# Transformer layer: the last chunk's queries in two parts of 256, and a later place for the weights' rounding

## What is computed

```python
x = x + attention(layernorm(x))          # 16 heads of 16, rope on q and k, causal, q/k/v/o biases
x = x + fp4_mlp(layernorm(x))            # 704 wide, silu(gate) * up, then down
# fp4_linear(x, w): x and w are rounded to FP4 (E2M1) in blocks of 16 with one scale each,
# and then multiplied in float32; the hidden layer h is rounded the same way before "down"
att = where(causal, q @ k.T / sqrt(16), -inf); y = softmax(att) @ v; attention = y @ Wo.T + bo
```

## Time and profile before

| | us |
|---|---|
| median of 3 runs | 1295.78 (1288.91, 1295.78, 1295.86) |
| the profiled execution's own time | 1292.66 |
| its span in the profile | 1290.9 |
| TensorE busy | 1203.7 (93%) |
| VectorE busy | 1093.9 (85%) |
| ScalarE busy | 755.4 (59%) |
| GpSimd busy | 476.9 (37%) |

### The profile page before, as it was taken

How to read it: one execution, slowest core, us unless ns; L and a number is a source line. 1 busy time by engine, 2 the same in 40 slices (tenths; PEclk the granted TensorE clock), 3 DMA queues, 4 the chain that set the end, 5 groups by cost and what they waited for, 6 DMA issues and landing times.

```text
span 1290.9 us, 40076 instructions
## 1 busy us (share of the span) xinstructions
PE 1203.7 (93%) x16718; PEld 669.9 (52%) x16718; DVE 1093.9 (85%) x2932; ACT 755.4 (59%) x1630; POOL 476.9 (37%) x501
## 2 busy tenths in 40 slices
PE   8679999899999899999999899989999999999967
PEld 7345454454555445545565465545645554545545
DVE  6799998889997998999469799899899999885366
ACT  5246776466565476575655457456656566676621
POOL 3945655544213132122345663311122123014345
PEclk9779999899999999999999999989999999999989
DMA  4735323302101101101044222121111200000000
GB/s 108 183 96 163 103 77 88 99 26 68 43 28 51 51 3 51 35 27 45 10 109 128 81 77 77 51 61 35 38 34 44 59 11 3 19 2 18 5 22 16
DMA packets 79504, 72.40 MB, mean 56 GB/s; under 512 B 25934, under 2 KB 65744, under 8 KB 79312
## 3 DMA queue, kind: packets, MB, share of 16 engines
q1 hardware_dynamic: 76296, 68.76, 19.7%
q10 hardware_dynamic: 3028, 1.09, 0.3%
HBM read 45.07 MB, written 24.35 MB: 54 GB/s over the span
## 4 chain that ended last, share of the span: by engine, by line
PE 60%; DVE 24%; DMA 4%; ACT 4%; issue 3%; POOL 3%; SPq 1%; ACTq 0%; POOLq 0%; DVEq 0%
PE bank L992 13%; PE bank L968 11%; PE bank L1004 10%; PE bank L947 10%; DVE piece_max L1371 8%; DVE bank L1368 7%; PE bank L1123 5%; PE bank L1063 4%; ACT prob L1257 3%; PE bank L1097 2%; PE bank L1071 1%; PE bank L1114 1%; DVE piece_max L1368 1%; DMA q_mem<-max_rows 1%; DMA a_mem<-in_L_attn_x 1%
## 5 line engine op out<-in xcount | busy, mean ns | idle before, releaser
L1257 ACT ACTIVATE prob<-bank 128x512 f32<-128x512 f32 (+3 forms) x1280 | 594.2, 541 | 269.7 <-PE bank L968 152.6
L1371 DVE TENSOR_REDUCE piece_max<-bank 128x1 f32<-128x512 f32 x768 | 487.3, 676 | 9.4 <-PE bank L947 7.9
L968 PE MATMUL bank<-q_mem,k_mem 99*32 99x512 bf16 (+12 forms) x5120 | 388.0, 344 | 15.5 <-DMA q_mem<-max_rows 11.3
L947 PE MATMUL bank<-k_mem,q_mem 96*32 96x512 bf16 (+14 forms) x5120 | 379.5, 346 | 10.3 <-DVE piece_max L1368 5.9
L992 PE MATMUL bank<-prob,V 128*32 128x512 f32 (+3 forms) x2560 | 294.8, 533 | 13.5 <-ACT prob L1257 9.1
L968 PEld LDWEIGHTS bank<-q_mem,k_mem 99*32 99x32 bf16 x5120 | 144.5, 97 | 166.7 <-issue 70.3
L947 PEld LDWEIGHTS bank<-k_mem,q_mem 96*32 96x32 bf16 x5120 | 134.1, 97 | 186.2 <-issue 104.4
L1596 POOL TENSOR_TENSOR c_mem<-c_mem 128x256 f32<-128x256 f32 (+2 forms) x74 | 85.4, 1155 | 380.1 <-DVE c_mem L1470 380.1
L1368 DVE CUSTOM_DVE_ANT_0 bank<-bank,past_keys 128x32 f32<-128x32 f32 (+15 forms) x512 | 208.1, 468 | 3.3 <-PE bank L947 3.2
L992 PEld LDWEIGHTS bank<-prob,V 128*32 128x32 f32 x2560 | 70.4, 110 | 65.8 <-ACT prob L1257 30.5
L973 PE MATMUL bank<-mask_kq,ident_h 128*32 128x64 bf16 (+3 forms) x2048 | 101.6, 201 | 0.0
(11 more groups left out here) (177 smaller groups left out, 1337.9 us busy)
## 6 DMA issues: line engine op xcount, KB each, us to landing
output_dram<-attn SPq DMA_DIRECT2D x28, 256.0 KB, 3.0
parts_dram<-a_mem SPq DMA_DIRECT2D x13, 512.0 KB, 3.8
q_mem<-parts_dram SPq DMA_DIRECT2D x32, 192.0 KB, 3.1
k_mem<-parts_dram SPq DMA_DIRECT2D x32, 192.0 KB, 3.6
q_mem<-parts_dram SPq DMA_DIRECT2D x32, 128.0 KB, 3.1
k_mem<-parts_dram SPq DMA_DIRECT2D x32, 128.0 KB, 3.4
c_mem<-in_L_attn_x SPq DMA_DIRECT2D x30, 128.0 KB, 2.2
out<-c_mem SPq DMA_DIRECT2D x30, 128.0 KB, 1.7
```

The costliest lines, as they stand in the source:

```text
L947: m = pe.matmul(b[COLUMNS * h:COLUMNS * (h + 1), of], q_rows(u)[0:TERM_ROWS, h, block * COLUMNS:(block + 1) * COLUMNS], k_rows(k0 // CHUNK ...
L968: mm = pe.matmul(b[k0:k0 + COLUMNS, since:CHUNK], k_rows(j // TPC, g)[:, h, first:first + COLUMNS], q_rows(u)[:, h, since:CHUNK], start=Tr ...
L1257: act.activation(prob[:, n % NP, off:CHUNK], bank_of("st", n)[:, off:CHUNK], ACT.Exp, scale=SCALE).then_inc(drained("st", n)[0], 1)
L1371: r = dve.tensor_reduce(most, scores, AX.X, ALU.max)
```

## The change

- The last chunk has 8 units in place of 4: units 28 to 31 are its four groups for queries 0 to 255, units 32 to 35 the same groups for queries 256 to 511. The first part sees 14 steps of 128 keys a unit, the second 16, all up to 256 queries wide; before there were 16 steps up to 512 wide.
- Queries and keys are dealt to `q_mem` and `k_mem` only once for both parts (`dealt`, `deal_of`); the maxima are made and placed for each part.
- The pieces on the diagonal are packed anew: 3 banks in the first part and 8 in the second, in place of 9 a unit; the other 48 pieces of a group are split 24 and 24.
- A tile of the last chunk waits for the four units of its own part (`tile_normalised`), so tiles 28 and 29 can start after units 28 to 31.
- In the last 8 units the steps may hold 5 banks in place of 3.
- `w` of SOONER_NS goes from 0 to -20000.

```diff
-SOONER_NS = dict(a=0, w=0, xn=10000, ...
+SOONER_NS = dict(a=0, w=-20000, xn=10000, ...
...
-    units = [(k, g) for k in range(CHUNKS) for g in range(NGROUPS)]
+    PARTS = 2
+    units = [(k, g) for k in range(CHUNKS - 1) for g in range(NGROUPS)]
+    queries = [(0, CHUNK)] * len(units)
+    for part in range(PARTS):
+        units += [(CHUNKS - 1, g) for g in range(NGROUPS)]
+        queries += [(part * CHUNK // PARTS, (part + 1) * CHUNK // PARTS)] * NGROUPS
...
-        steps += [(u, j, max(0, j - c * TPC) * P) for j in range((c + 1) * TPC)]
+        low, high = queries[u]
+        steps += [(u, j, max(low, (j - c * TPC) * P)) for j in range(c * TPC + high // P)]
...
+        blocks = list(range(queries[u][0] // COLUMNS, queries[u][1] // COLUMNS))
+        pieces += [(u, [(0, n, j * BANK, BANK, j, False)]) for n in blocks for j in range(c)]
+        while blocks:
+            of = [blocks.pop(0)]
+            for n in reversed(blocks):
+                if n != BLOCKS - 1 and sum((n_ + 1) * COLUMNS for n_ in of + [n]) <= BANK:
+                    of.append(n)
+            blocks = [n for n in blocks if n not in of]
...
+    dealt = CHUNKS * NGROUPS
+    def deal_of(u):
+        return u if u < dealt else u - NGROUPS * ((u - dealt) // NGROUPS + 1)
...
     def rehearse_probabilities():
+            in_flight = 5 if u >= len(units) - 2 * NGROUPS else ST_IN_FLIGHT
...
+    def units_of(t):
+        k, i = tiles[t]
+        return [u for u in range(k * NGROUPS, len(units)) if units[u][0] == k and queries[u][0] <= i * P < queries[u][1]]
-    def chunk_normalised(k):
+    def tile_normalised(t):
+        k, _ = tiles[t]
         if by_transfers(k):
             return [("y", k * NGROUPS // 2 + p) for p in range(NGROUPS // 2)]
-        return [("drain", "oT", k * NGROUPS + g) for g in range(NGROUPS)]
+        return [("drain", "oT", u) for u in units_of(t)]
...
             def probabilities():      # TensorE
-                        masked = j >= c * TPC
+                        masked = j * P >= c * CHUNK + queries[u][0]
...
-                            mm = pe.matmul(b[k0:k0 + COLUMNS, since:CHUNK], ..., q_rows(u)[:, h, since:CHUNK], ...)
+                            mm = pe.matmul(b[k0:k0 + COLUMNS, since:end], ..., q_rows(u)[:, h, since:end], ...)
...
             def probabilities():      # ScalarE
-                        act.activation(prob[:, n % NP, off:CHUNK], bank_of("st", n)[:, off:CHUNK],
+                        act.activation(prob[:, n % NP, off:end], bank_of("st", n)[:, off:end],
...
             def outputs():
-                    act.activation(attn[:, :], bank[O_BANK][:, :], ACT.Copy).then_inc(o_copied, 1)
+                    of = slice(*queries[u])
+                    act.activation(attn[:, of], bank[O_BANK][:, of], ACT.Copy).then_inc(o_copied, 1)
...
             def turn_output(b, u):
-                for i in range(TPC):
+                for i in range(queries[u][0] // P, queries[u][1] // P):
```

More of the change, by code:

```diff
@@ L371, in rehearse_maxima @@
             keys, own = sum(part[3] for part in parts), parts[0][5]
-            yield from plan.wait([("deal q", u, len(RUNS) - 1)] + ([("deal k", u, len(RUNS) - 1)] if own else [])
+            yield from plan.wait([("deal q", deal_of(u), len(RUNS) - 1)] + ([("deal k", deal_of(u), len(RUNS) - 1)] if own else [])
                                  + ([("place", u - 2, 2)] if u >= 2 else [])
@@ L408, in rehearse_values @@
             of = k - k % NCHUNKS + j // TPC
-            yield from plan.step("pe", ("pv", m), 1.67 * (CHUNK - off) + 26,
+            yield from plan.step("pe", ("pv", m), 1.67 * (queries[u][1] - off) + 26,
                                  [("drain", "st", GROUP * m + 3), ("drain", "v", (of * TPC + j % TPC) // PAIR)]
@@ L413, in rehearse_values, with turned_before @@
                 old = [("o store" if by_transfers(units[u - 1][0]) else "oT", u - 1)] if u else []
-                yield from plan.step("act", ("o copy", u), 493, [("pv", m)] + old)
+                yield from plan.step("act", ("o copy", u), 80 + 0.807 * (queries[u][1] - queries[u][0]), [("pv", m)] + old)
                 plan.start(rehearse_normalising(u), SOONER_NS["norm"])
         plan.give(O_BANK, ("o copy", len(units) - 1))
+    def turned_before(u):
+        return u > 0 and not by_transfers(units[u - 1][0])
     def rehearse_normalising(u):
@@ L422, in rehearse_normalising @@
             yield from plan.wait(old)
-            yield from plan.through(("oT", u), 440, "dve", 335, [("o copy", u)], old,
-                                    ("dve", ("recip", u), 170) + ((("drain", "oT", u - 1),) if g else ()))
+            share = PARTS if k == CHUNKS - 1 else 1
+            yield from plan.through(("oT", u), 440 / share, "dve", 60 + 275 / share, [("o copy", u)], old,
+                                    ("dve", ("recip", u), 70 + 100 / share) + ((("drain", "oT", u - 1),) if turned_before(u) else ()))
             return
@@ L487, in rehearse_tiles @@
             yield from plan.wait(until=lambda: not tiles_c or all(
-                name in plan.end for name in chunk_normalised(tiles[tiles_c[0]][0])))
+                name in plan.end for name in tile_normalised(tiles_c[0])))
             if tiles_c:
@@ L915, in sync_engine @@
             in_time(constants(), *(project(z) for z in range(len(pairs))), *(store_parts(z) for z in range(len(pairs))), *(key_ones(c) for c in range(NCHUNKS)),
-                    weights(), *(deal(u) for u in range(len(units))),
+                    weights(), *(deal(u) for u in range(dealt)),
                     *(place_maxima(sp, at, u) for u in range(len(units)) if not placed_by_scalar(u)),
@@ L1082, in turn_y @@
                 k, i = tiles[t]
-                for g in range(NGROUPS):
-                    at.wait_ge(*drained("oT", k * NGROUPS + g))
+                for u in units_of(t):
+                    at.wait_ge(*drained("oT", u))
                 return turn(b, Y[:, k % 2, i, :])
@@ L1250, in probabilities @@
                 for m, (u, j, off) in enumerate(steps):
+                    end = queries[u][1]
                     for h in range(GROUP):
```

43 lines of the change are left out of this document (21 added, 22 removed).

## The result

The changed kernel takes 1284.4 us (median of 6 runs, 1282.0 to 1286.4) against 1294.2 for the kernel before on the same chip: a ratio of 0.9916, 95% interval 0.9896 to 0.9937, some 11 us faster. The forecast was 1286.5, so the number came out right, 2.1 us off. The interval leaves out 1, so a change of under 1% could be told from none here.

What follows compares the result with a forecast made beforehand. The prediction took TensorE's work plus its idle time as the bound. From the profiled execution, 1292.7 - 16.4 + 20.2 - 2 - 7 + 2 - 3 = 1286.5 us; whole range 1274 to 1304, the forecast's own 1279 to 1294.

Steps and rivals of the forecast that it cites:

- The tail with two tiles: After the last copy, two tiles remain instead of four: the tail takes 44.3 us in place of 60.7, -16.4.
- The same work in the attention: Two tiles moved into the last chunk's attention, where TensorE has nothing to spare, lengthen it at 10.1 us each: +20.2.
- the filling: Tiles 28 and 29 start late, so some of their TensorE work fills holes in the tail: -7 (0 to -14).
- the 2 us of idle time: In units 30 and 31, more ready work and 5 banks take most of TensorE's 3.0 us idle: -2 (0 to -3).
- The length of the last chunk: Sign to look for in the profile: the last chunk's attention, 211 us before, takes 225 to 233.
- Finer steps: Last chunk's steps of 256 instead of 512: exponentials hidden by ScalarE's idle time, values groups and copies mostly covered, +2.
- The bound of 16.4: Upper limit for the last chunk's halved steps: all 14 us of values groups exposed, and the copies at full cost.
- Weights: Later weight steps should remove TensorE's waits of 4.8 and 4.1 us for GpSimd's rounding: -3 (-8.9 to +7.0).
- the placing late: Rival: at unit starts in the last chunk, probabilities wait for placed maxima, four more starts at 3.6 us: 1301, chance 0.12.
- Not in time: Rival: tiles 28 and 29 hardly start before the last copy, the tail stays at 60.7: 1291.7, chance 0.11.
- All paid: Rival: tiles 28 and 29 done wholly beside the second part, no filling, nothing from the weights: 1296.5, chance 0.18.
- the good fit: Rival: 14 us of the early tiles' work in the tail's holes and both weight waits gone: 1273.5, chance 0.17.

Runs made afterwards that it cites:

- parts_old_front: The halved last chunk and early tiles with w = 0, copy costed 493 or 287 ns to keep the old order until the last chunk: 1310.9 us, ratio 1.0107 to before.
- no_early_tiles: The changed kernel, but tiles 28 to 31 all wait for all eight units of the last chunk: 1291.4 us, ratio 0.9967 to the kernel before.
- w_only: The kernel before with only the weights' entry of SOONER_NS set to -20000: 1284.0 us, ratio 0.9912.
- short_exps: The changed kernel, exponentials of the last 8 units computed for half their columns, so not a valid layer: 1280.6 us, ratio 0.9866 to the kernel before.
- w20_copy480: The kernel before with w = -20000 and the values' bank copy costed 480 ns in the plan in place of 493: 1304.3 us, ratio 1.0064.
- parts_only: The changed kernel with the weights' entry of SOONER_NS back at 0: 1320.0 us, ratio 1.0185 to the kernel before.
- copy_cost: The kernel before with the values' bank copy costed 493.18 ns in the plan in place of 493, same instructions: 1312.1 us, ratio 1.0121.

## Why the prediction was right, and where it was not

- *The bound* (TensorE's work plus its idle time): held; both sides of it moved as the tables show.
- *The tail with two tiles, -16.4, to 44.3*: 44.1 in parts_old_front, where both early tiles are done before it. Right for such a tail. In the changed kernel it is 47.0, since tile 29 reaches into it, within the 44 to 50 that were named.
- *The same work in the attention, +20.2, and the filling, -7*: together with the tail and the 2 us of idle time these terms gave -5.2. Measured by itself (the changed kernel against no_early_tiles), -7. Tile 28's load came 36.6 us before the last copy, tile 29's 12.9: late, as argued (the pair of the 73 us had its other tile loaded at 1020.8 already), and more of their work fell into the holes than I took: idle time of the tail 12.4, where 44.3 less two tiles less 7 would leave 17.
- *The length of the last chunk, 225 to 233*: 246.8. Wrong. In w_only it is 232.1 already, against 211.7 before, because fewer tiles had been served before it began; I did not foresee that. Finer steps make it 239.8, the early tiles 246.8. With the old front it is 244.1, where the finer steps cost more.
- *Finer steps, +2*: the mis-sized term. It measured 7 us (no_early_tiles against w_only); with the old front, where the other terms without a filling give +1.8, the parts cost 14 us, so the steps would be some 12. The step that did not hold is "cutting one in two costs 0.03 us ... ScalarE is idle for 75 us in these four units, which hides either" and "some 0.25 us that are normally covered by the next matmuls ... I take 1.5". Room of ScalarE as a sum over a unit hid that in the second half of the chunk, where no maxima are left, ScalarE sets the pace of the steps, as short_exps shows. A whole step takes it 4 x 0.50 = 2.0 us there, two halves 2.2, and TensorE's own work is 1.7 us in both. How much of the 7 us this makes was not measured. The bound of 16.4 held it in both; the value taken was from units 28 and 29, which have maxima, and not from 30 and 31, which are what becomes longer.
- *Weights, -3*: with this order -11.4 (0.0088 x 1294.2). The mechanism that I gave, the two waits of 4.8 and 4.1 us, is not it. The first of these became 3.3 us after, the second went, others took their place, and the idle time to 260 us did not change. The time was won from chunk 1 to chunk 6, 11 us of idle time, in many waits, and another order with the same w (w20_copy480) loses it. The last sentence of the prediction named this as the thing that no row bounds: the middle moved by more than the ends.
- *The rivals*: the placing late did not come; the longest wait for placed maxima from 260 us on is 0.4 us. No placing was blocked in the last chunk either: the operation that took 2.03 us in the earlier trace rows takes at most 0.18 from 989 us on. "Not in time" did not come. "All paid" is what parts_old_front does, with some 10 us of the finer steps on top. (The sum of the good fit gives 1273.6, not 1273.5.)
- The forecast was -5 (tiles) + 2 (steps) - 3 (weights), so -6 us; the runs give -7 + 7 - 11, so -11, against -9.8 between the medians (1294.2 less 1284.4). I took 5 us too little cost for the steps, and too little gain for the tiles (2) and the weights (8). That the total is 2 us off is in good part luck: these errors partly cancel, and the largest hangs on one order. Under another order in front, with w = 0, the same two parts come out at 1320.0.

What stays open: whether the later weights gain on average, and why the halved chunk costs 14 us in one order, 8 in another and nothing in a third. The parts of the last chunk, early tiles and finer steps, were split up in one order only. Executions of one order also differ: up to unit 27's end parts_only took 1051.0 us in its profile and copy_cost 1040.7, with VectorE's instructions in the same order.

## What to carry to other kernels

Where a greedy plan orders the engines, test an edit against orders that differ by a tie: here 0.18 ns in one cost moved the kernel by 1.2%, more than the whole change. Moving a task from a tail made of waits into a stretch that its engine fills pays, by the sums here, only for what still reaches into the tail's holes: it gained 7 us where tile 29 lay half in the tail, and no gain was seen where both tiles were done before it. Before halving a step, look at the engine that feeds it in the stretch where it is the pace, not at its idle time over the whole.

## What the runs showed of the hardware that was not expected

- ScalarE's exponentials of 256 columns come 0.26 to 0.30 us apart over 32 of them, against 0.50 for 512; at 0.27 a pair of halves costs 0.04 us more than a whole, although the mean durations are 386 and 606 ns.
- TensorE's recorded busy time rises with its waits. A float32 values' group of 256 columns is recorded with 0.64 us, yet the next matmuls start 0.46 us after it (0.43 in short_exps); when TensorE waits, the open end of the last matmuls counts as busy. With the same matmuls the changed kernel records 1211.3 us and short_exps 1203.8.
